# Cross-attention of a float32 decoder: 18 of 24 probability tiles turned by VectorE in 32x32 blocks and moved by DMA, and the softmax denominator applied after the weighting

## The reference

```
scores[b,h,t,s] = q'[b,h,t,:] . ctx_rot[b,s,:]        # 1500 context positions s, 64 channels, 16 heads
p               = softmax(scores, axis=s)
c[b,h,t,:]      = sum_s p[b,h,t,s] * ctx_pos[b,s,:]   # weighted context, 64 channels
out[b,t,:]      = sum_h c[b,h,t,:] @ cm[h]            # folded value and output weights, then residual + layer norm
```

## Time and profile before

| | us |
|---|---|
| median of 3 runs | 1667.23 |
| the 3 runs | 1664.79, 1667.23, 1677.47 |
| span of the profiled execution | 1666.3 |
| TensorE, VectorE, ScalarE, GpSimd busy in the span | 1627.4, 1113.9, 749.9, 239.1 |

### The profile page before, as it was taken

The page is one execution under the profiler, slowest core; times in us unless marked ns, Lnnn a source line. Parts: engine busy times, 40 slices in busy tenths (PEclk is TensorE's granted clock), DMA queues, the critical chain, the costliest instruction groups (busy, mean ns, idle before and its releaser), DMA issues.

```text
span 1666.3 us, 35653 instructions
## 1 busy us (share of the span) xinstructions
PE 1627.4 (98%) x15234; PEld 1104.8 (66%) x15234; DVE 1113.9 (67%) x1974; ACT 749.9 (45%) x1297; POOL 239.1 (14%) x428
## 2 busy tenths in 40 slices
PE   9999999999999899999999999999999999999998
PEld 5575367777755666655377777764566767777765
DVE  3735899999566763266899999435445289999623
ACT  2223366666413641144366666312444366666411
POOL 0011300000010313011200000010455000000030
PEclk9999999999999999999999999999999999999999
DMA  8302020000040011051020000050300220000010
GB/s 280 86 13 83 1 78 2 2 2 2 2 187 1 2 59 40 1 133 48 1 97 2 2 2 2 4 240 0 64 1 1 114 89 2 2 2 2 2 44 11
DMA packets 35522, 71.10 MB, mean 43 GB/s; under 512 B 25359, under 2 KB 29775, under 8 KB 31433
## 3 DMA queue, kind: packets, MB, share of 16 engines
q1 hardware_dynamic: 35240, 68.71, 12.6%
q10 hardware_dynamic: 126, 0.11, 0.0%
HBM read 68.36 MB, written 0.46 MB: 41 GB/s over the span
## 4 chain that ended last, share of the span: by engine, by line
PE 89%; DVE 6%; ACT 2%; POOL 1%; issue 1%; DMA 1%; SPq 0%; DVEq 0%; POOLq 0%; ACTq 0%
PE ps L1122 14%; PE ps L1135 14%; PE ps L1035 13%; PE ps L1501 9%; PE ps L361 9%; PE ps L946 3%; PE ps L2599 3%; PE ps L1150 3%; PE ps L528 2%; PE ps L1961 2%; PE ps L956 1%; POOL arena L1795 1%; PE ps L2626 1%; PE ps L982 1%; PE ps L967 1%
## 5 line engine op out<-in xcount | busy, mean ns | idle before, releaser
L1236 ACT ACTIVATE arena<-ps,softmax_stats 128x1500 f32<-128x1500 f32 x168 | 253.8, 1511 | 193.0 <-DVE softmax_stats L1317 190.8
L1135 PEld LDWEIGHTS ps<-arena,ctx_pos 125*64 125x64 f32 x4608 | 222.3, 137 | 58.4 <-issue 55.4
L1122 PE MATMUL ps<-ident,arena 64*125 64x64 f32 x4032 | 239.1, 271 | 1.9 <-ACT arena L1236 1.6
L1135 PE MATMUL ps<-arena,ctx_pos 125*64 125x128 f32 (+1 forms) x4608 | 240.5, 262 | 0.0
L1122 PEld LDWEIGHTS ps<-ident,arena 64*125 64x125 f32 x4032 | 226.8, 185 | 17.0 <-issue 13.5
L1035 PE MATMUL ps<-ctx_feat,arena 64*128 64x500 f32 x1008 | 230.5, 590 | 0.0
L1243 ACT COPY arena<-ps 125x512 f32<-125x512 f32 x336 | 172.5, 600 | 77.9 <-PE ps L1122 77.9
L1315 DVE TENSOR_REDUCE softmax_stats<-ps 128x1 f32<-128x500 f32 x252 | 170.6, 678 | 49.0 <-PE ps L1035 48.6
L361 PE MATMUL ps<-arena 128*128 128x256 f32 x736 | 174.7, 383 | 3.5 <-DVE arena L1630 1.2
L1328 DVE TENSOR_SCALAR arena<-arena,softmax_stats 128x1500 f32<-128x1500 f32 x168 | 168.3, 1002 | 5.9
L1501 PE MATMUL ps<-x_feat,arena 128*128 128x448 f32 (+1 forms) x416 | 167.9, 549 | 1.2 <-DVE arena L1613 1.2
(11 more groups left out here) (324 smaller groups left out, 1931.7 us busy)
## 6 DMA issues: line engine op xcount, KB each, us to landing
ctx_pos<-in_ctx SPq DMA_DIRECT2D x1, 2688.0 KB
arena<-in_L1f_gate SPq DMA_DIRECT2D x1, 2304.0 KB, 12.1
arena<-in_L1f_up SPq DMA_DIRECT2D x1, 2304.0 KB, 17.0
arena<-in_L1f_down SPq DMA_DIRECT2D x1, 2304.0 KB, 7.8
arena<-in_L0a_Wq SPq DMA_DIRECT2D x1, 2048.0 KB, 10.9
arena<-in_L0a_Wc SPq DMA_DIRECT2D x1, 2048.0 KB, 18.8
arena<-in_L0x_Wq SPq DMA_DIRECT2D x1, 2048.0 KB, 9.9
arena<-in_L0x_Wo SPq DMA_DIRECT2D x1, 2048.0 KB, 8.3
```

The source lines that it names most:

```text
L1122: m = nc.tensor.transpose(c.ps[0:LP, turn_bank(i, k, r), n * 64:(n + 1) * 64], probs[i % 2][e][rows, l * LP:(l + 1) * LP], c.ident[rows, r ...
L1135: m = nc.tensor.matmul(y[r * 64:(r + 1) * 64, lo:hi], c.ctx_pos[:, j, l, e, :], pT[i % 2][:, lo // 64:hi // 64, LT * e + l, :], start=(l = ...
L1236: nc.scalar.activation(probs[i % 2][e].rearrange("p (k l) -> p k l", k=3), sc[e], ACT.Exp, bias=low[:, i % 4, e:e + 1], accum_out=total[:, ...
```

## The change

The denominator is no longer multiplied into the probabilities. `turn_blocks(i, e)` has VectorE transpose 32x32 blocks of the unscaled probabilities from SBUF to SBUF, 12 tiles for e = 0 and 6 tiles for e = 1; since VectorE turns only within 32 partitions, four DMAs a unit, issued by SyncE, then bring the blocks of each group of 32 rows (`frm`) to the 128 partitions of `moved_to`. Each of them copies 32 partitions x 4 x 576 floats into 128 partitions x 576 floats. TensorE turns the other 6 tiles of e = 1 (`BY_PE`), 12 transposes instead of 48, and ScalarE copies them (two copies of 125x384). In the probability buffer a tile now takes 128 columns (`LQ`), 125 of them used; the source of the block transposes is read as `(l q g) -> g l q`, with g = 4, that is every fourth float, and written without gaps.

The reciprocals go to GpSimd, which multiplies them into an identity (`diag`), TensorE spreads them over the 64 rows of channels with a matmul by `ones` (`spread`), ScalarE copies that out (`keep_spread`), and GpSimd multiplies the kept context by it when it places it (`place_context`). `keep` moves from VectorE to ScalarE. The exponential of e = 1 is two operations, 1000 and 500 columns, so that `score(i, 0)` of the next unit waits for the first alone; VectorE adds the two sums. The prefetch moves from SyncE to ScalarE's queue.

```
-    pT = [c.at(o["PT"] + i * LT * 256, LT * 256, LP).rearrange("p (r s q) -> p r s q", r=2, q=64) for i in range(2)]
-    probs = [[c.at(o["P"] + (2 * i + e) * L, L) for e in range(2)] for i in range(2)]
+    blocks = [c.at(o["TT"][i], 4 * RUN).rearrange("p (g n) -> p g n", g=4) for i in range(2)]
+    moved_to = [c.at(o["PT"] + i * 4 * RUN, 4 * RUN).rearrange("p (g n) -> p g n", g=4) for i in range(2)]
+    probs = [[c.at(o["P"] + (2 * i + e) * LT * LQ, LT * LQ) for e in range(2)] for i in range(2)]
...
     def _(sp):
-        prefetch(sp)
+        for i in range(NU):
+            sp.wait_ge(blocked[1].handle, blocked[1].at(i + 1))
+            if i >= 2:
+                sp.wait_ge(pv_mm.handle, pv_mm.at(i - 1))
+            for frm in range(4):
+                sp.dma_start(moved_to[i % 2][:, frm, :],
+                             blocks[i % 2][32 * frm:32 * frm + 32, :, :]).then_inc(moved[i % 2].handle, 16)
...
         def score(i, k):
             if i > 0 and k == 0:
-                for e in range(2):
-                    pe.wait_ge(exped[e].handle, exped[e].at(i))
+                pe.wait_ge(exped[0].handle, exped[0].at(i))
+                pe.wait_ge(exped[1].handle, exped[1].at(2 * i - 1))
+            if i > 0 and k == 2:
+                pe.wait_ge(exped[1].handle, exped[1].at(2 * i))
...
         def weigh(i):
-            pe.wait_ge(a_in.handle, a_in.at(4 * (i + 1)))
-            pe.wait_ge(d_in.handle, d_in.at(2 * (i + 1)))
+            pe.wait_ge(b_in.handle, b_in.at(2 * (i + 1)))
+            pe.wait_ge(moved[i % 2].handle, moved[i % 2].at(64 * (i // 2 + 1)))
+            if i > 0:
+                pe.wait_ge(kept.handle, kept.at(i))
...
-            for k in turn_order(i - 1):
-                turn(i - 1, k)
+            turn(i - 1)
+            spread(i - 1)
...
         def exp(i, e):
+            nc.scalar.activation(to[:, 0:2], frm[:, 0:2], ACT.Exp, bias=low[:, i % 4, 1:2],
+                                 accum_out=total[:, i % 4, 1:2]).then_inc(*exped[1].next())
+            nc.scalar.activation(to[:, 2], frm[:, 2], ACT.Exp, bias=low[:, i % 4, 1:2],
+                                 accum_out=rest[:, i % 4:i % 4 + 1]).then_inc(*exped[1].next())
...
+        for i in range(NU + 2):
+            if i >= 3:
+                keep(i - 3)
+            if i >= 2:
+                copy_turned(i - 2, 0)
+                copy_turned(i - 2, 1)
+                keep_spread(i - 2)
             if i < NU:
                 exp(i, 0)
                 exp(i, 1)
...
     def _(dve):
+        def turn_blocks(i, e):
+            dve.wait_ge(exped[e].handle, exped[e].at((1 + e) * (i + 1)))
...
+            n = BY_PE * e
+            nc.vector.transpose(blocks[i % 2][:, :, 32 * LT * e:32 * (LT + (LT - n) * e)].rearrange("p g (l h) -> p g l h", h=32),
+                                probs[i % 2][e][:, n * LQ:].rearrange("p (l q g) -> p g l q", g=4, q=32)).then_inc(*blocked[e].next())
...
-        for i in range(NU + 1):
...
+        for i in range(NU):
+            rowmax(i)
+            if i == 0:
+                cm_out(2)
+            turn_blocks(i, 0)
+            turn_blocks(i, 1)
+            invert(i)
```

More of the change, by code:

```diff
@@ L1102, in _, with turn @@
         out_of_context(3)
[L1104 to L1113 removed]
+        def turn(i):
+            pe.wait_ge(exped[1].handle, exped[1].at(2 * i + 1))
+            if i == 0:
@@ L1170, in _ @@
         project(1)
-        for k in range(3):
-            turn(NU - 1, k)
+        turn(NU - 1)
+        spread(NU - 1)
         project(2)
```

188 lines of the change are left out of this document (98 added, 90 removed).

## The result

The changed kernel takes 1707.63 us (median of 4 runs, 1704.17 to 1716.22), the kernel before 1670.59 in the runs beside it. The ratio is 1.024, 95% interval 1.019 to 1.029: slower by some 37 us, on the side forecast and inside the forecast's range, but 21 us less than the 1729 us forecast. The profiled execution is the slowest of the four: 1716.22 us, span 1714.4.

A forecast was written before the change was run, and what follows sets the result against it. TensorE was taken to bound the kernel, with VectorE next. Units of 8.92 us instead of 8.10 give + 23.1 us a stage, - 2.6 outside, three times + 20.5: 1729 us; own range 1700 to 1755, widened 1566 to 1780.

The forecast's parts named there:

- The bound: Steady cross-attention loop: TensorE bounds the kernel before; after the change VectorE's queue sets the unit, TensorE idling 2.3 us.
- TensorE's part: TensorE's work in a loop unit: scores 2.57, weighted sum 2.77, transposes 0.69, spread 0.23; 6.6 us with 0.3 for waits.
- The price of the transposes: VectorE's two strided block transposes in each unit: 3.35 and 1.75 us, dense time plus 1.037 ns a column.
- Rival B: VectorE's transposes pay only 0.75 ns a column for the step: 8.26 us a unit, 1675 us; chance 0.14.
- The queue: VectorE's operations in a loop unit, back to back with no idle time: 8.92 us, the new unit length.
- GpSimd's four small operations: GpSimd in the loop gets four small operations a unit where it had two: no cost.
- The exponential in two operations: ScalarE's split exponential of e = 1 in the loop buys nothing, since VectorE reads the scores later.
- The DMAs: Four DMAs a unit moving turned blocks stay hidden: 8.6 us needed at most, 10.1 us available; no cost.
- The loads on ScalarE's queue: Weight loads issued from ScalarE once a stage, 3 to 5 times 0.56 us beside VectorE's work in unit 0: nothing.
- Head and tail: Outside a stage's loop, before the first projection and in the last unit: together - 2.6 us a stage.
- Rival A: VectorE's block transposes run at the dense rate, 1.75 and 0.96 us: 1564 to 1605 us; chance 0.33.
- Rival C: Forecast's mechanism plus TensorE's granted clock falling in every second loop unit: + 48 us, 1777 us; chance 0.11.

The follow-up runs named there:

- run 1: Changed kernel with its block transposes reading 32 neighbouring floats instead of every fourth, so the output is not the attention: 1605.9 us, ratio 0.962.
- run 4: Changed kernel with four buffers instead of two for the kept sums and kept spread, waits two units further back: 1695.1 us, ratio 1.017.
- run 6: Changed kernel in which only a stage's first two units move turned blocks by DMA, later ones reading what these left: 1705.3 us, ratio 1.025.
- run 8: As run 7, with the next stage's weight loads issued by SyncE behind the last unit's moves: 1842.9 us, ratio 1.106.
- run 10: Changed kernel, strided transposes kept, with four buffers, one exponential for the second batch and weight loads behind the last unit's moves: 1674.0 us, ratio 1.005.
- run 5: Changed kernel with ScalarE issuing the next stage's weight loads one in every fourth unit instead of all in the first: 1717.9 us, ratio 1.030.
- run 2: Changed kernel with its block transposes reading every second float instead of every fourth, output again not the attention: 1602.8 us in one run.
- run 3: Changed kernel with the second batch's exponential as one operation again, without VectorE's addition of the two sums: 1698.1 us, ratio 1.020.
- run 7: Changed kernel with first-batch scores reading the context strided so the larger transpose reads densely, plus four buffers and one second-batch exponential: 1855.8 us, ratio 1.114.
- run 9: As run 8, with the first batch's context reordered once when the first attention stage copies it out of PSUM: 1616.7 us, ratio 0.971.
- run 11: As run 9, with VectorE's addition and reciprocals of a unit moved behind the next unit's reductions: 1604.0 us, ratio 0.965.
- run 12: As run 11, with the second batch's exponential in two operations again: 1610.5 us, ratio 0.965.

## Why the prediction was right, and where its size was off

**The bound.** Right. VectorE took over, TensorE idles before the scores (81.6 us in all), and the unit is VectorE's queue.

**TensorE's part.** Right in the sum: scores 2.79, weighted sum 2.84, transposes 0.87, spread 0.44 us by the timeline, 6.6 us back to back once their overlaps of 0.1 are taken off; run 1's shortest units are 6.69. The parts were off: I had 0.69 for the transposes and 0.23 for the spread, and the 0.3 us that I had set aside for waits covers the difference.

**The price of the transposes** is the term that was mis-sized. I took 3.35 and 1.75 us, the dense time plus a whole column time for the step; they took 2.97 and 1.53, 0.60 us less a unit. The lower bound of L2024 in the earlier trace rows, 0.7 ns a column, was nearly the value itself (0.78 and 0.72 by run 1), and my allowance of another third of a nanosecond, for columns fetched in the fixed part, was mostly not there: from 768 to 1536 columns each further one costs 1.88 ns with the step and 1.046 without, 0.84 more where I took 1.037. Rival B had 2.9 and 1.5. I gave it 0.14 and my own figure 0.42; the row pointed at B, and I had added to it. (B's 0.75 ns is not the 0.7 of the row either; with 0.7 it would have come to 8.14 us a unit.)

**The queue.** With the measured transposes my sum gives 8.92 - 0.60 = 8.32 us. Run 4, in which VectorE hardly waits, has 8.25 to 8.28, so the rest of the queue was right to 0.05 us. The changed kernel has 8.42: the 0.15 more are VectorE's wait for the exponential. I had reckoned 0.04 us between L1382's end and the turning from the earlier trace rows, where ScalarE's exponential started 0.12 us after the reduction; now the copy of the spread is ahead of it and waits for GpSimd. That GpSimd's four small operations cost nothing was the second step that failed: some 0.15 us in each unit and 0.5 in every seventh, 15 to 17 us in all (run 4: 15 by the loops' last 72 steps, 17.2 by the idle time before the transposes).

**Why B did not come true all the same.** Its 1675 us are 32 us short. Its loop was 8.26 us and run 4, without the wait, has 8.25 to 8.28. The loops were to sum to 671.6 us and do to 703.6. Against 8.27 us a unit, the 72 last steps take 16 us more (the wait for GpSimd and the one unit of 9.77), the third units 10, the second 1, and the first 4 more than B's 9.1 (10.3 to 10.6): together 31.

**The exponential in two operations.** I had said that it buys nothing. In a clean unit it costs 0.2 us, in one with slow scores it saves; on balance removing it is 9 us faster in the changed kernel by the loops (703.6 to 695.0). So VectorE's bound made it worth nothing as a gain, as I had said, but it was not free.

**The DMAs.** Hidden in the steady loop, as forecast (run 6). But the weighted sum does wait for a DMA in the third units, 8.6 us in all, which my own list had as a sign that the transfer time was too short; it was the loads beside the moves that I had left out. The loads on ScalarE's queue I had priced as issue time alone, and not as traffic against the moves: 4.6 to 4.7 us in each of two stages, a slow TensorE in the weighted sum included. Behind the stage's last moves they delay no third unit (runs 8 and 10). That they can't simply be spread out is run 5.

**Head and tail.** The three stretches outside the loops give - 7 to - 10 us when the stretch at the lower clock is taken out; my sum had - 2.6 a stage, - 7.8, though in L0 the first projection ran at the lower clock (5.36 us, 3.67 in the earlier trace rows):

```profile
443.63 5.36 PE L1188 MATMUL ps<-arena 128*64 128x256 f32 x32 [1.96 <-issue]
```

**Rival A** (dense rate) is what runs 1 and 2 built: 1606 and 1603 us against its 1564 to 1605. As the forecast of this kernel it was wrong, since its transposes read with a step of four floats. The sentence of the Trainium skill, "Vector Engine (DVE) Microarchitecture Reference", on the reshape front-end (one element per cycle and lane) agrees with runs 1 and 2, in which a transpose has the rate of the plain dense operations (1.046 ns a column, 1.037 by the earlier trace rows); with a step of four floats it doesn't hold.

**Rival C** (the clock). The granted clock in the loops was 0.94 to 0.96. As a price for each second unit it did not occur: VectorE bounds, and most slow scores hide. It showed where cover was gone: the third units, one unit of L2 with 9.77 us, 19 units in run 3, 14 in run 10.

So the forecast's sign and bound came out by the mechanism given. Its loops were 725.1 us, measured are 703.6. The 21.5 us come apart as 49 too much for the transposes (81 times 0.60) and 4 for the rest of the queue (81 times 0.05), against 31 that I had not counted: 16 in the 72 last steps (the wait for GpSimd and the unit of 9.77), 10 in the third units, 1 in the second and 4 in the first. So the total was nearer than its largest term, and that is luck: with the transposes at their true price my sum gives 1680 us, below the forecast's own range of 1700 to 1755, and costs that I had put at nothing brought the time back into it.

## What to carry to other kernels

Before work is moved to another engine, look at the step of what it reads: every second float cost VectorE nothing, every fourth some 0.75 ns a column, and TensorE 1.8 ns a column of a float32 matmul; reorder once, where the data is copied anyway. A bound from a nearby row ("at least 0.7 ns") is the best first value too, unless another row speaks for more. And price a background load by what it delays, not only by what it takes to issue.

## What the runs showed of the hardware

VectorE's block transpose of float32 runs at 1.046 ns a column with a step of one or two floats, and at 1.88 with a step of four (from 1536 against 768 columns, runs 1 and 2 and the changed kernel).

TensorE pays for a step of four floats in its moving operand from SBUF: the 12 score records of a unit, of which six have it, take 5.59 us, without it 2.8 (runs 7 and 9).

Reading PSUM with a step of four floats cost neither copying engine anything. The reordering copies of run 9, 496 columns with the step beside 500 without, VectorE and ScalarE:

```profile
L686 DVE COPY ctx_feat<-ps 64x500 f32<-64x500 f32 x6 | 4.1, 682 | 0.1
L686 DVE COPY ctx_feat<-ps 64x496 f32<-64x496 f32 x6 | 4.0, 665 | 0.4 <-PE ps L525 0.3
...
L631 ACT COPY ctx_feat<-ps 64x500 f32<-64x500 f32 x6 | 3.4, 571 | 0.1
L631 ACT COPY ctx_feat<-ps 64x496 f32<-64x496 f32 x6 | 3.4, 566 | 2.6 <-PE ps L525 2.5
```

The Trainium skill, "Advanced Engine Details and Errata", section on PSUM cachelines, gives PSUM lines of 8 bytes and says that patterns that aren't contiguous slow matmuls. No run here shows matmuls that write so; for these reads by VectorE and ScalarE there is no such price. Perhaps ScalarE's exponential could then do the reordering of run 9 by its own reads; that is untried.

What stays open: why the granted clock fell in some stretches and not in others. The stretch ahead of L3's loop had 0.60 in the profiled execution of the changed kernel and 1.00 in that of run 3, with the same code there. In the loops it was 0.91 to 0.96 in the versions with strided transposes, where TensorE idles 1.1 us a unit or more, and 0.98 to 0.99 in runs 9, 11 and 12, where it idles 0.5 to 0.6; but also 0.95 to 0.97 in runs 1, 2, 7 and 8, where it idles 0.2 to 0.4.
